# Softmax row sums and their running adds, the split of the row maxima, and the group comparisons of the router on other engines and banks, in a fused attention and mixture-of-experts layer

## The reference

```python
scores = jnp.einsum('bqhrd,bkhd->bhrqk', q, k) * scale
scores = jnp.where(causal, scores, jnp.finfo(scores.dtype).min)
probs = jax.nn.softmax(scores, axis=-1)
y = jnp.einsum('bhrqk,bkhd->bqhrd', probs, v)
...
grp = sc.reshape(T, N_GROUP, E // N_GROUP)
group_scores = jax.lax.top_k(grp, 2)[0].sum(-1)
_, gidx = jax.lax.top_k(group_scores, TOPK_GROUP)
```

## Time and profile before

| what | value |
|---|---|
| median of 3 runs | 410.92 us (407.57 to 411.22) |
| profiled execution, its own time | 407.81 us |
| its span, first to last instruction | 405.5 us |
| mean granted TensorE clock | 0.987 |
| busy: PE / DVE / ACT / POOL | 95% / 71% / 57% / 75% |

### The profile page before, as it was taken

How to read it: one execution, slowest core, us unless ns; L and a number is a source line. 1 busy time by engine, 2 the same in 40 slices (tenths; PEclk the granted TensorE clock), 3 DMA queues, 4 the chain that set the end, 5 groups by cost and what they waited for, 6 DMA issues and landing times.

```text
span 405.5 us, 6914 instructions
## 1 busy us (share of the span) xinstructions
PE 385.0 (95%) x2104; PEld 257.6 (64%) x2104; DVE 289.0 (71%) x711; ACT 231.9 (57%) x450; POOL 303.7 (75%) x354
## 2 busy tenths in 40 slices
PE   8989999999999969999999999999999999999992
PEld 8664555645445625434566888778877888788871
DVE  6996998675967894545528876597765777566764
ACT  4555355664664635756574655865665655565552
POOL 6117959999799995997879887598855988376651
PEclk9999999999999998999999999999999999999996
DMA  7367370074500500500000000000000000000000
GB/s 220 52 158 126 50 200 3 0 107 146 77 5 2 79 1 4 78 4 2 2 2 0 2 2 0 2 26 1 2 0 2 26 1 2 1 0 27 0 0 26
DMA packets 9905, 14.54 MB, mean 36 GB/s; under 512 B 1232, under 2 KB 5520, under 8 KB 9488
## 3 DMA queue, kind: packets, MB, share of 16 engines
q1 hardware_dynamic: 9584, 13.49, 16.4%
q10 hardware_dynamic: 288, 0.64, 0.5%
HBM read 6.26 MB, written 1.05 MB: 18 GB/s over the span
## 4 chain that ended last, share of the span: by engine, by line
PE 72%; DVE 12%; POOL 7%; issue 4%; ACT 2%; DMA 2%; SPq 0%; POOLq 0%; DVEq 0%; ACTq 0%
PE ps L1299 9%; PE ps L1300 9%; PE ps L1301 9%; PE ps L1413 7%; PE ps L1426 7%; PE ps L1392 6%; PE ps L1495 5%; PE ps L1497 4%; PE ps L1496 4%; DVE nmax_h L1144 3%; PE ps L1436 3%; POOL probs L808 2%; DMA qst<-q_lo 2%; DVE nm L1157 2%; PE ps L1309 1%
## 5 line engine op out<-in xcount | busy, mean ns | idle before, releaser
L888 POOL TENSOR_TENSOR silu<-silu,cwb 128x512 f32<-128x512 f32 x80 | 102.5, 1292 | 36.1 <-ACT silu L1018 32.0
L808 POOL TENSOR_TENSOR probs<-probs 128x1024 f32<-128x1024 f32 (+3 forms) x64 | 106.3, 1687 | 19.7 <-ACT probs L988 10.3
L1144 DVE TENSOR_REDUCE nmax_h<-ps 128x1 f32<-128x512 f32 (+3 forms) x152 | 91.7, 655 | 30.8 <-PE ps L1395 23.7
L988 ACT ACTIVATE probs<-ps 128x512 f32<-128x512 f32 (+1 forms) x152 | 80.3, 577 | 56.6 <-PE ps L1413 38.0
L1216 DVE TENSOR_TENSOR ps<-silu,ps 128x512 f32<-128x512 f32 (+1 forms) x84 | 57.8, 694 | 33.7 <-POOL silu L888 28.7
L1223 DVE TENSOR_TENSOR h_lo<-ps,h_hi 128x512 fp32r<-128x512 f32 (+1 forms) x84 | 57.2, 686 | 22.7 <-ACT h_hi L1030 21.9
L1018 ACT ACTIVATE silu<-ps 128x512 f32<-128x512 f32 x80 | 47.8, 597 | 39.7 <-PE ps L1301 33.6
L1030 ACT ACTIVATE h_hi<-ps 128x512 fp32r<-128x512 f32 (+1 forms) x84 | 50.0, 597 | 27.2 <-DVE ps L1216 26.2
L1299 PE MATMUL ps<-xT_hi,w_hi 128*128 128x512 f32 x164 | 65.2, 397 | 0.0
L1301 PE MATMUL ps<-xT_hi,w_lo 128*128 128x512 f32 x164 | 64.5, 393 | 0.0
L1300 PE MATMUL ps<-xT_lo,w_hi 128*128 128x512 f32 x164 | 64.4, 393 | 0.0
(11 more groups left out here) (187 smaller groups left out, 516.8 us busy)
## 6 DMA issues: line engine op xcount, KB each, us to landing
qst<-q_hi SPq DMA_DIRECT2D x14, 256.0 KB, 5.6
qst<-q_lo SPq DMA_DIRECT2D x7, 256.0 KB, 6.8
x_sb<-in_attn_x SPq DMA_DIRECT2D x4, 256.0 KB, 6.5
raw<-in_ffn_w_gate SPq DMA_DIRECT2D x1, 1024.0 KB, 5.1
raw<-in_ffn_w_up SPq DMA_DIRECT2D x1, 1024.0 KB, 5.2
raw<-in_ffn_w_down SPq DMA_DIRECT2D x1, 1024.0 KB, 4.8
kst<-k_hi SPq DMA_DIRECT2D x6, 128.0 KB, 5.0
result<-x_sb SPq DMA_DIRECT2D x3, 256.0 KB, 2.3
```

The source lines that it names most:

```text
L808: nc.gpsimd.tensor_tensor(into, into, probs[:, BUF[n, kt], j:end, cols], ALU.add).then_inc(added, 1)
L888: nc.gpsimd.tensor_tensor(silu[:, k % HRING, :], silu[:, k % HRING, :], cwb[:, m % 2, t // ET, :], ALU.mult).then_inc(scaled_ready, 1)
L988: nc.scalar.activation(probs[:, BUF[n, kt], j:j + w, at:at + cols], bank(full)[:, 0:w * cols].rearrange("p (w c) -> p w c", w=w), ACT.Exp) ...
L1144: nc.vector.tensor_reduce(nmax_h[:, n % 2, i, j:j + w, h], bank(full)[:, 0:w * keys].rearrange("p (w k) -> p w k", w=w), AX.X, ALU.max, ne ...
```

## The change

The row sums: `SUM_FROM` and its helpers go. A block, long or short, has one sum, that begins at key tile 0, so a long block adds 7 tiles instead of 5, and `ones` runs once a block (8 times instead of 16). The heads are divided in 3 and 1 (`SPLIT`, `ADDERS`): GpSimd adds heads 0 to 2 in the buffer as before, in one instruction per tile; the sum of head 3 lies in a PSUM bank. ScalarE copies its first tile there (`seed`), VectorE adds the others, the bank being operand and result. Before the last tile ScalarE copies back the columns that this tile doesn't reach (`sum_copy`, 384 columns), and VectorE's last add writes the remaining 128 columns to the buffer. The bank is held from `seed` to that last add.

The maxima: `nm_split` takes a bank itself (before, `shift` took it), VectorE waits for the bank's turn, reduces into it, and subtracts with the first operand in the bank. The reduction into `left` is now made in short blocks as well.

The router: step 3 moves from VectorE (2 instructions) to GpSimd (3). `ROUTE_RANK` goes from (4.5, 100, 121, 142) to (5.5, 98, 121, 142). `bank_turn` becomes a function of the engine; the many lines that only pass `pe` to it are left out here.

```diff
-SUM_FROM = {TPC: (0,), 2 * TPC: (0, 3, 6)}
-PARTS = ((0, 2), (2, REP))
+ADDERS = ("POOL", "DVE")
+SPLIT = (3,) * NB
...
-ROUTE = (("POOL", 90), ("DVE", 120), ("POOL", 25), ("DVE", 60), ...
+ROUTE = (("POOL", 90), ("DVE", 120), ("POOL", 25), ("POOL", 95), ...
...
-ROUTE_RANK = (4.5, 100, 121, 142)
+ROUTE_RANK = (5.5, 98, 121, 142)
...
-        step("DVE", ("nm_split", n), 45, n + 1, *[("max", *ev[1:]) for ev in steps], n >= 1 and ("shift", n - 1))
-        step("PE", ("shift", n), 60, n + 1, ("nm_split", n), bank=1, until=("shift_copy", n))
+        step("DVE", ("nm_split", n), 55, n + 1, *[("max", *ev[1:]) for ev in steps], n >= 1 and ("shift", n - 1), bank=1, until=("shift_copy", n))
+        step("PE", ("shift", n), 60, n + 1, ("nm_split", n))
...
+                if kt == 0 and SPLIT[n] < REP:
+                    step("ACT", ("seed", n), 22 + (REP - SPLIT[n]) * 41, rank - 0.1, *[e for e in exps if 1 in parts_of(e)], bank=REP - SPLIT[n], until=("add", n, kts(n) - 1, 1))
+                if kt:
+                    step("POOL", ("add", n, kt, 0), 18 + SPLIT[n] * cols * 215 // 1000, rank - 0.1, ("pv", n, 0),
+                         *[e for e in exps if 0 in parts_of(e)], kt > 1 and ("add", n, kt - 1, 0))
+                    step("DVE", ("add", n, kt, 1), 15 + (REP - SPLIT[n]) * cols * 105 // 1000, rank - 0.1, *[e for e in exps if 1 in parts_of(e)],
+                         ("add", n, kt - 1, 1) if kt > 1 else ("seed", n), kt == kts(n) - 1 and ("sum_copy", n))
+                if kt == kts(n) - 2:
+                    step("ACT", ("sum_copy", n), 22 + (REP - SPLIT[n]) * 31, rank - 0.1, ("add", n, kt, 1), ("pv", n, 0))
+        step("PE", ("ones", n), 10 + CH * 17 // 100, n + 2.9, *(("add", n, kts(n) - 1, part) for part in range(len(ADDERS))), bank=1, until=("recip", n))
+        step("DVE", ("recip", n), 170, n + 2, ("ones", n))
...
+                    elif r == 3:
+                        other = gscore[:].unsqueeze(2).to_broadcast([P, TPC, EG, EG])
+                        own = gscore[:].unsqueeze(3).to_broadcast([P, TPC, EG, EG])
+                        link(nc.gpsimd.tensor_tensor(above[:], other, own, ALU.subtract))
+                        link(nc.gpsimd.tensor_scalar(ties[:], above[:], 0.0, None, ALU.is_equal))
+                        last = nc.gpsimd.tensor_scalar(above[:], above[:], 0.0, None, ALU.is_gt)
...
+                elif kind == "seed":
+                    n = ev[1]
+                    act.wait_ge(exp_ready, max(EXP["exp", *e[1:]] for e in p2_steps(n) if e[2] == 0 and 1 in parts_of(e)))
+                    bank_turn(act, ev)
+                    nc.scalar.activation(late_sums(n), probs[:, BUF[n, 0], SPLIT[n]:, :], ACT.Copy).then_inc(copied, 1)
...
+                    bank_turn(dve, ev)
+                    left = bank(ev)[:, 0:TPC * REP].rearrange("p (i j) -> p i j", j=REP)
+                    nc.vector.tensor_reduce(left, heard, AX.X, ALU.min)
...
+                elif kind == "add":
+                    _, n, kt, part = ev
...
+                    into = probs[:, BUF[n, 0], j:end, cols] if last else late_sums(n)[:, :, cols]
+                    nc.vector.tensor_tensor(into, late_sums(n)[:, :, cols], probs[:, BUF[n, kt], j:end, cols], ALU.add).then_inc(added[part], 1)
...
-                        nc.vector.tensor_tensor(above[:], other, own, ALU.is_gt)
-                        last = nc.vector.tensor_tensor(ties[:], other, own, ALU.is_equal)
```

More of the change, by code:

```diff
@@ L111, in p2_steps, with part_heads @@
     return out
+def part_heads(n, part):
+    return (SPLIT[n], REP) if part else (0, SPLIT[n])
 def parts_of(ev):
-    return {part for part, (j, end) in enumerate(PARTS) if ev[3] < end and j < ev[3] + ev[4]}
-def first_of(n, kt):
-    return max(f for f in SUM_FROM[kts(n)] if f <= kt)
-def last_of(n, f):
-    return max(kt for kt in range(kts(n)) if first_of(n, kt) == f)
+    return {part for part in range(len(ADDERS)) if ev[3] < part_heads(ev[1], part)[1] and part_heads(ev[1], part)[0] < ev[3] + ev[4]}
 def buffers():
@@ L141, in buffers @@
             at[n, kt], was[n, kt], held[own] = own, held[own], (n, kt)
-            if kt == last_of(n, first_of(n, kt)):
-                turn.append(first)
-    name = {own: k for k, own in enumerate(turn)}
-    return {x: name[own] for x, own in at.items()}, was, [held[own] for own in turn]
+        turn.append(first)
+    name = {at[NB - 1, kt]: k for k, kt in enumerate((1, 2, 3, 0))}
+    return {x: name[own] for x, own in at.items()}, was
 WARM = 14
@@ L239, in chunk_of, with leaves @@
         return CPB * b + c
-    def leaves(user):
+    def leaves(user, parts=range(len(ADDERS))):
         if user is None:
@@ L245, in leaves @@
         n, kt = user
-        return [("ones", n, kt)] if kt == first_of(n, kt) else [("pv", n, kt), *(("add", n, kt, part) for part in range(len(PARTS)))]
+        return [("pv", n, kt), *(("add", n, kt, part) for part in parts)] if kt else [("ones", n)]
     step("SP", ("x_load",), 320, 0)
@@ L388, in lies_over @@
     def lies_over(row):
-        return leaves(LEFT[row // REP])
+        return leaves((NB - 1, (1, 2, 3, 0)[row // REP]))
     for k in range(NU):
@@ L458 @@
 RSTD = count("POOL", "xn_rstd", "post_rstd", "post_rstd2", "fin_rstd")
-ADD = count("POOL", "add")
+ADD = [{ev: k + 1 for k, ev in enumerate(e for e in PLAN[engine] if e[0] == "add" and e[3] == part)} for part, engine in enumerate(ADDERS)]
 MUL = count("POOL", "mul")
@@ L579, in sums, with late_sums @@
             return bank(("down", MT * m))
+        def late_sums(n):
+            return ps[:, BANK["seed", n]:BANK["seed", n] + REP - SPLIT[n], :]
         def rows_left(engine, row):
-            n, kt = LEFT[row // REP]
-            engine.wait_ge(pv_done, PV["pv", n, kt])
-            if kt == first_of(n, kt):
-                engine.wait_ge(ones_done, ONES["ones", n, kt])
-            else:
-                engine.wait_ge(added, max(ADD["add", n, kt, part] for part in range(len(PARTS))))
+            kt = (1, 2, 3, 0)[row // REP]
+            engine.wait_ge(pv_done, PV["pv", NB - 1, kt])
+            for part in range(len(ADDERS)):
+                engine.wait_ge(added[part], ADD[part]["add", NB - 1, kt, part])
         def tail_tiles(half):
@@ L639, in build @@
         pv_done = sem("pv_done")
-        added = sem("added")
+        added = [sem(f"added{part}") for part in range(len(ADDERS))]
         ones_done = sem("ones_done")
@@ L1429, in _ @@
                 elif kind == "ones":
[L1430 to L1434 removed]
+                    n = ev[1]
+                    for part in range(len(ADDERS)):
+                        pe.wait_ge(added[part], ADD[part]["add", n, kts(n) - 1, part])
+                    bank_turn(pe, ev)
                     for j in range(REP):
[L1436 to L1437 removed]
+                        last = nc.tensor.matmul(bank(ev)[LAT * j:LAT * j + LAT, :], ones[:], probs[:, BUF[n, 0], j, :], start=True, stop=True)
                     last.then_inc(ones_done, 1)
```

209 lines of the change are left out of this document (101 added, 108 removed).

## The result

| what | before | after |
|---|---|---|
| median | 409.53 us (20 runs, 407.57 to 411.46) | 407.38 us (20 runs, 403.25 to 412.15) |
| ratio, 95% interval | | 0.991 [0.9885, 0.9934] |
| profiled execution | 407.81 us | 408.77 us |
| its span, granted clock | 405.5 us, 0.987 | 406.7 us, 0.975 |

The medians are 2.2 us apart (0.5%), and the ratio, which goes by all runs but the slow one of 412.15, stands for 3.7 us (0.9%). The forecast was 8 us (409.4, the middle of the four times shown before, less 401.5). The 20 runs of after lie in two groups: 8 of 403.25 to 405.12 us (middle 403.9) with a mean clock of 0.985 to 0.993, and 12 of 406.75 to 412.15 (middle 408.3) with 0.963 to 0.985.

What follows compares the result with a forecast made beforehand. TensorE's queue was taken to bound the kernel: 405.5 - 6.2 - 5.1 - 1.5 - 0.6 + 2.5 + 3.0 = 397.6 us span, 399.9 for the profiled execution, 401.5 us for the median; range 394 to 412.

Steps and rivals of the forecast that it cites:

- The bound: Whole kernel: TensorE's queue sets the time, busy for 385.0 of 405.5 us; other engines' work counts only where it delays TensorE.
- the clock of 1.00 there: Sign that the forecast holds: TensorE's granted clock at 1.00 in 140 to 160 us.
- (a): Rival: the split waits for its bank, the hole at 147 us stays, only ones steps pay; 408.1 us, chance 0.12.
- (d): Rival: the split's subtraction still stretches, one operand in the bank or not; 407 us, chance 0.04.
- Rival (b): VectorE becomes the bound from 20 to 140 us; 418 us, chance 0.14 with what leads towards it.
- One bank less: Changes of block, 3 banks left for passes 1 and 2: +3.0 us, with coarser adds and hand-overs.
- GpSimd's adds: GpSimd's adds of heads 0 to 2, up to 3.49 us each: counted 0, though norm and router steps behind wait longer.
- waits for maxima or exponentials grow: Sign that the forecast is wrong: TensorE's waits for these grow from tenths to several us.
- split's holes and their clock: Split of the maxima, 140 to 200 us: two large TensorE holes go, -5.1 us, and half clock behind, -1.5 us.
- ones steps: TensorE, 4 long blocks: each loses one step over 512 and one over 256 columns, counted in full, -6.2 us.
- VectorE's adds: VectorE, 40 to 60 us: the adds of blocks 0 and 1 have no cover, +2.5 us, bounds 0 and +12.
- comparisons: Router's step 3, moved from VectorE to GpSimd: -0.6 us, bounds -1.1 and +1.

Runs made afterwards that it cites:

- `keys_in_plan`: Changed kernel, replanned with the planner told that a transfer of keys takes 5.5 us instead of 2.2; 401.27 us, ratio 0.9806.
- `load_later`: Changed kernel, with the load of the 1 MB of weights moved behind the shift's transfer on SyncE's queue; 406.42 us, ratio 0.9908.
- `both_later`: Changed kernel, with the weights' load moved behind the shift's transfer and chunk 1's norm two exponentials later on ScalarE; 407.67 us, ratio 0.9937.
- `split_by_reductions`: Kernel before, in its own order, with the split's subtraction replaced by two reductions, no bank needed; 402.2 us, ratio 0.9797.
- `sbuf_operand`: Changed kernel, with the first operand of the split's subtraction back in SBUF, the bank still waited for; 407.32 us, ratio 0.9937.
- `two_sums_less`: `split_by_reductions` without the ones matmuls of the second and third sum but for one column each; 399.41 us, ratio 0.9762.
- `adds_one_column`: Changed kernel, in its own order, with VectorE's 40 adds cut to one column each; 407.12 us, ratio 0.9904.
- `reductions_added`: `split_by_reductions` plus 40 VectorE reductions of the adds' sizes where the adds would stand; 409.34 us, ratio 1.0.
- `comparisons_moved`: `split_by_reductions` with the router's step 3 on GpSimd, replanned; 403.7 us, ratio 0.9864.
- `pool_adds_one_column`: Changed kernel, in its own order, with GpSimd's 40 adds cut to one column a head; 401.75 us, ratio 0.9821.
- `bank_held`: `split_by_reductions`, replanned with one of the eight banks held from the second chunk's transposes to the last exponential; 408.88 us, ratio 1.0009.
- `keys_moved`: Changed kernel, with block 4's first passes moved behind ready work of block 2 on TensorE; 404.24 us, ratio 0.9857.
- `norm_later`: Changed kernel, with the norm of chunk 1's attention output moved two exponentials later on ScalarE's queue; 407.29 us, ratio 0.9912.

## Why the prediction was right on the split and wrong on the whole

**What was right.** The bound: TensorE's queue sets the time, and the mixture's phase stayed as it was (185.5 and 186.2 us from the last ones step to the last matmul, 399.5 - 214.0 and 400.8 - 214.6). The split: its wait was the largest single price of before; I counted 6.6 us (5.1 and 1.5) and the split alone gives 8.0. (That VectorE's products "in the same phase" don't stretch was read from the mixture's phase, not from attention; the forecast of 0.2 us came true all the same.) The subtraction takes 174 ns in all eight places, the ones step has 64 instructions, and no wait of TensorE above 2 us is left in 140 to 160 us; the clock of 1.00 there, forecast beside it, was 0.74. Rivals (a) and (d) fell: TensorE waited for the split for 0.6 us in all, and VectorE for the split's bank for 0.2 us, once. Rival (b) fell too: without the adds' columns the time is the same within the interval.

**What was wrong** is the term "One bank less", +3.0 "for this, the coarser adds and the hand-overs together". I priced it by waits that each would be short, with a range of nothing to 1.4 us at each of 7 changes of block. What is missing in it is the order: the planner deals out every queue anew from costs, banks and due times, and I took the new order to be as good as the old. With the same instructions in another order, and with the same adds, hand-overs and banks held, `keys_in_plan` takes 401.27 us instead of 407.38, so these are not dear by themselves. In the trace the first order shows two places:
- It put pass 1 of block 4 where its keys were still on their way: 2.8 us of hole, and 3.4 us of half clock. Moving it by hand gives 404.24 us, but the intervals of the two ratios overlap, two new holes stand in its place, and the gain isn't shown to be this hole's.
- It left the norm's factor behind an add of 3.46 us, with the norm's bank next on TensorE: 1.3 us of hole, and 10.2 us of half clock in the profiled run and none in those of `load_later` and `both_later`. I had written that "every norm or router step behind it waits that much longer" and yet counted 0, because I looked for who waits for GpSimd's adds and not for who waits for what stands behind them. With the adds cut short 5.6 us come back by the medians; with the factor alone ahead of the add the ratio stays (0.9907), and in `keys_in_plan` the same queue hardly holds TensorE up. So the long add is a part of it, together with where pass 1 stands, and not a price by itself.

Part of the miss is the execution's and no fault of a term: the lower eight runs of after (403.9 in the middle) are 2.4 us above the forecast, the upper twelve (408.3) 6.8.

My own sign for being wrong was "waits for maxima or exponentials grow"; what grew was a wait for a transfer and one for a bank, which I hadn't listed, and the clock was a term only where I gave it back, never one that new holes could cost.

**The other terms,** as far as the runs size them:

| term | predicted | measured | by |
|---|---|---|---|
| split's holes and their clock | -6.6 | -8.0 in the order of before; 0 to -1.1 in that of after, not clear of noise | `split_by_reductions`, `sbuf_operand` |
| ones steps | -6.2 | -1.4 to -2.8, not clear of noise | `two_sums_less` |
| VectorE's adds | +2.5 | 0 where planned for, +7.1 to +8.3 where not | `adds_one_column`, `reductions_added` |
| comparisons | -0.6 | +1.5 to +2.7, replanned | `comparisons_moved` |
| GpSimd's adds | 0 | +3.6 to +5.6, the half clock behind the second hole included | `pool_adds_one_column` |
| one bank | in the +3.0 | +6.7 to +8.7, replanned | `bank_held` |

These don't sum, as each replanned run has another order and a hole can cost more through the clock than by its length. "TensorE has no gap there to lose it in, so I count all of it" failed for the ones steps: work taken from the fullest engine closes up only until the next producer (here probabilities and queries) is the late one.

With 5.5 us for the keys in the planner the change makes 401.27 us, beside the 401.5 predicted. That is partly luck: the split gains more than I wrote and the ones steps less. Beside the split I had the rest of the change at -1.3 us net (-6.2 + 2.5 + 3.0 - 0.6), and in this order it is worth nothing that can be told (0.9806 against 0.9797 and 0.983).

**What stays open.** Whether `bank_held` loses by the bank or by the order made for it. How the order's cost divides between the two holes, the banks and the half clock, and why one order runs with and without the 10.2 us at half. Why keys and factor moved together (406.57) are worse than the keys' move alone (404.24). And `keys_in_plan` is one order out of many: its first changed places are nearly those of `keys_moved`, but that the rest of its gain comes from the keys' figure isn't shown.

## What to carry to other kernels

Where a planner makes the order, a change of costs and banks is a change of order, and the order can be worth as much as the change: before the time of such a change is believed, look in the new order for each transfer and bank whose user now stands sooner, and compare the planner's figure for it with the landing time on the page (2.2 and 7.4 us here). Giving the planner a better figure is no gain by itself: two of three kernels kept their order to the last step, so compare the orders before the times. Where the times of one kernel lie in two groups (403.9 and 408.3 us in the middle here), compare group with group: a median of six runs moves with the share of either, and a profile shows one of the two only. A single stall is best repaired alone first: 8.0 us came from two reductions that touched no queue, no bank and no other engine.

## What the runs showed of the hardware

- A VectorE instruction of 16 columns with both operands in SBUF waited through two GpSimd adds and a part of a third (5.42 us in before), not one; up to 2.09 us in `sbuf_operand`. With an operand in a bank (after) it took 174 ns, and as a reduction (`split_by_reductions`) 186 ns at the median, 188 at most.
- The length of a hole doesn't tell what the clock costs behind it: after 4.1 us it was at half for 3.4 us in before, after 2.8 us for 3.4 us in after, and after 1.3 us for 10.2 us. The same hole with 1.6 us had 10.2 us of half clock behind it in `norm_later` and none in `load_later`. In `split_by_reductions` the clock was at half for 3.4 us from 94 us on with TensorE busy for 13.73 of the 14 us ahead of it. After's runs go from 403.25 us at a mean clock of 0.993 to 409.21 us at 0.967.
- A transfer of 128 KB within SBUF took 4.9 us from issue to landing in the median (`k_hi`, six of them in after), and 7.4 us with three to five others under way in 82 to 97 us; without the 1 MB of weights behind it 7.3 and 7.0 us (`load_later`).
